# A routed feed-forward layer behind graph attention: which earlier sum tiles 4 and 5 wait for before they are added into the output

## The chip, the cores and the metric

The kernel runs on one core of a Trainium2 chip. The metric is the device time of one execution in microseconds (us); lower is better. The time before is the median of three runs.

## What is computed

```python
# x: (64, 128, 512), adj: (64, 128, 128), all fp32; 8192 tokens of 512 numbers
x = x + attention(layernorm(x), bias=adj + adj, Wq, Wk, Wv, Wo)    # 16 heads, within each block of 128 tokens

h = layernorm(x)                                                   # 8192 tokens
scores = maximum(h @ gate_W + gate_b, 1e-4)
p = softmax(scores)                                                # over 8 experts
topk_idx = top_k(p, 2)
w = maximum(p, 0.1) at the two chosen experts, divided by their sum
y = einsum('bsd,edf->bsef', h, expert_W) + expert_b
x = x + einsum('bsef,bse->bsf', y, comb) / 2                       # comb: w at the two chosen experts, else 0
```

## The kernel before

**Phase one** (`phase_a`) does the attention for 64 blocks of 128 tokens. It writes x after attention into the DRAM tensor `out`, and it scatters every normalised token twice into `x_lists`, once into the list of each of its two experts. A row of `x_lists` holds the 512 numbers, the token's number and its eight combination weights. At its end DVE fills the small table `tab` with three integers for each of the 135 tiles of phase two: the tile's expert, its first row in `x_lists`, and a count, described below.

**Phase two** (`phase_b`, L1201 to L1347) goes over the lists in 135 tiles of 128 rows (`TILES = 135`, 8192 x 2 / 128 = 128 and 7 spare ones), expert by expert. Below, tiles are counted from 0. Each engine has its own program, and the loops run over 6 tiles (`N`) per turn `g`, unrolled in Python; `tile(g, off)` is tile number 6g + off. There are 6 buffers for the gathered rows (`xg`) and their `token` and `comb`, and 3 (`R`) for `xgT_hi`, `xgT_lo`, `ps_x`, `ps_y` and `yt`.

- ACT gathers tile n into `xg` by a DMA (L1288), after a wait for the transposes and the `token` and `comb` copies of tile n-6 (L1286, L1287). In one step it first copies the transposed tile n from `ps_x` to `xgT_hi` (L1281) and then issues the gather of tile n+5.
- PE transposes tile n+2 into `ps_x` (L1266) between the three matmuls for each of four chunks of tile n into `ps_y` (L1260, L1261, L1262). Tile n's matmuls wait for `xgT_lo` of tile n (L1254) and for the addition of `yt` of tile n-3 (L1256).
- DVE takes in one step L1300 (`xgT_lo` = `ps_x` - `xgT_hi`) for tile n+2, then for tile n L1309 (`yt` = `ps_y` + bias, after a wait for the landing of the sum of tile n-3, whose buffer it takes, L1308) and L1312 (`yt` times the weight).
- POOL takes in one step the copies of `token` and `comb` for tile n+2 (L1330, L1331) and then the sum of tile n: an indirect DMA which adds the rows of `yt` into the rows `token` of `out` (L1343). It increments `added[n % 3]` by 16 when all of it has landed.

A token stands in two lists, so two sums of different experts can meet in a row of `out`, and an addition must not start before the other one has landed. Two tiles of one expert never share a token. The third number of `tab` says how far `added` of the previous tile's buffer must have come: 16 * ((n-1) // 3), which leaves the previous tile's own sum out, and 16 more where tile n-1 belongs to another expert, which takes it in. The value is at least 16 from tile 4 on. The wait order before each sum is:

```python
if t.after(2 * R):                       # L1335: from tile 6 on
    need = pool.value_load(tab[0:1, 2, bass.ds(t.count(), 1)], ...)
    hold(added[(j - 3) % R], 16 * tile(g, j - 3).turn(R) + 16)     # the sum of tile n-2 has landed
    hold(added[(j - 2) % R], need)                                 # what the table asks of tile n-1's buffer
elif t.after(1):                         # tiles 1 to 5
    pool.wait_ge(added[(j - 2) % R], 16 * tile(g, j - 2).turn(R) + 16)   # the sum of tile n-1 has landed
hold(y_step, t.count(2, 2))              # yt of tile n is complete
```

`hold` (L1317 to L1320) is a wait followed by an increment of a counter of POOL's own. The functions that the diff touches follow with the line numbers of the profile.

Of the kernel before, what the change touches and what calls it, by code (L numbers as in the profile page):

```python
# [1200 lines left out]
def phase_b(nc, v):  # L1201
# [5 lines left out]
    R = RING  # L1207
# [3 lines left out]
    with mem:  # L1211
# [20 lines left out]
        def tile(g, off):  # L1232
            return Item(g, N, off, TILES)

        def turns(body):
            for g in range(-1, TILES // N + 2):
                body(g)
# [3 lines left out]
        @block.tensor  # L1241
        def _(pe):
            def body(g):
                for j in range(N):

                    ahead, t = tile(g, j + 2), tile(g, j)
                    if ahead.valid:
                        pe.wait_ge(xg_in[ahead.ring(N)], 16 * ahead.turn(N) + 16)
                        if ahead.after(R):
                            pe.wait_ge(xgT_lo_done, ahead.count(1, 1 - R))  # L1250
                    if t.valid:
                        r = t.ring(R)
                        e = pe.value_load(tab[0:1, 0, bass.ds(t.count(), 1)], min_val=0, max_val=E - 1)
                        pe.wait_ge(xgT_lo_done, t.count(1, 1))  # L1254
                        if t.after(R):
                            pe.wait_ge(y_step, t.count(2, 1 - 2 * R))  # L1256
                    for c in range(DC):
                        if t.valid:
                            hi, lo = (we[:, bass.ds(e * (2 * DC * D) + (DC * i + c) * D, D)] for i in range(2))
                            nc.tensor.matmul(ps_y[r][:, :], xgT_hi[:, r, c, :], hi, start=c == 0, stop=False)  # L1260
                            nc.tensor.matmul(ps_y[r][:, :], xgT_hi[:, r, c, :], lo, start=False, stop=False)  # L1261
                            last = nc.tensor.matmul(ps_y[r][:, :], xgT_lo[:, r, c, :], hi, start=False, stop=c == DC - 1)  # L1262
                            if c == DC - 1:
                                last.then_inc(y_full, 1)
                        if ahead.valid:
                            last = nc.tensor.transpose(ps_x[ahead.ring(R)][:, P * c:P * c + P], xg[:, ahead.ring(N), P * c:P * c + P], ident)  # L1266
                            if c == DC - 1:
                                last.then_inc(xgT_full, 1)
            turns(body)
# [45 lines left out]
        @block.gpsimd  # L1315
        def _(pool):
            def hold(semaphore, value):  # L1317

                pool.wait_ge(semaphore, value)
                pool.sem_inc(poolb_held, 1)  # L1320

            def body(g):
                for j in range(N):
                    t = tile(g, j + 1)
                    if t.valid:
                        r, m = t.ring(R), t.ring(N)
                        hold(xg_in[m], 16 * t.turn(N) + 16)
                        if t.after(N):
                            hold(added[r], 16 * t.turn(R) - 16)
                        nc.gpsimd.tensor_copy(token[:, m, :], xg[:, m, D:D + 1]).then_inc(meta_done, 1)  # L1330
                        nc.gpsimd.tensor_copy(comb[:, E * m:E * m + E], xg[:, m, D + 1:W]).then_inc(meta_done, 1)  # L1331
                    t = tile(g, j - 1)
                    if t.valid:
                        r, m = t.ring(R), t.ring(N)
                        if t.after(2 * R):  # L1335

                            need = pool.value_load(tab[0:1, 2, bass.ds(t.count(), 1)], min_val=16, max_val=16 * (TILES // R + 1))
                            hold(added[(j - 3) % R], 16 * tile(g, j - 3).turn(R) + 16)
                            hold(added[(j - 2) % R], need)
                        elif t.after(1):  # L1340
                            pool.wait_ge(added[(j - 2) % R], 16 * tile(g, j - 2).turn(R) + 16)
                        hold(y_step, t.count(2, 2))
                        pool.indirect_dma_start(out=out, out_offset=bass.IndirectOffsetOnAxis(ap=token[:, m, :], axis=0),  # L1343
                                                in_=yt[:, r, :], in_offset=None, compute_op=ALU.add).then_inc(added[r], 16)
            turns(body)
            for r in range(R):
                pool.wait_ge(added[r], 16 * (TILES // R))  # L1347
# [42 lines left out]
```

## Time and profile before

| | |
|---|---|
| median of 3 runs | 1660.67 us (1660.43 to 1661.73) |
| the profiled execution | 1662.81 us |
| its span, first to last instruction | 1661.0 us |
| mean granted TensorE clock | 0.970 |
| PE busy | 1550.8 us (93%) |
| DVE, ACT, POOL busy | 1215.8, 955.9, 974.0 us |
| phase two | from about 1195 us on |
| sums into `out` (L1343), 135 | first at 1210.2, last at 1654.2 us |

The profile tells for each instruction when it started, how long it took and what ended the idle time of its engine before it. `PE` is the TensorE, `DVE` the VectorE, `ACT` the ScalarE, `POOL` the GpSimd. A granted clock of 1.00 is 2.4 GHz on the TensorE and 0.50 is 1.2 GHz. The duration of an indirect DMA on POOL is POOL's own work in issuing it; the transfer itself goes on behind it.

### The profile page before, as it was taken

The page shows a single profiled execution, that of the slowest core. Times are in us where ns is not written, and L with a number is a line of the kernel's source. Part 1 is how long each engine was busy: PE and PEld are TensorE (multiplying, and loading weights), DVE is VectorE, ACT ScalarE, POOL GpSimd, SP SyncE. Part 2 cuts the span into 40 slices and gives each one's busy share as a digit, 9 for nine tenths or more (in the row PEclk, how much of TensorE's full clock was granted, in tenths as well). Part 3 has the DMA queues.
Part 4 walks back from the last instruction along what each step waited for, and adds up shares of the span by engine and source line. Part 5 has one row for each costly group of instructions (what it writes and reads, how often), then busy time and mean ns, then how long its engine had stood idle before and what let it go on. Part 6 is the DMA issues. An engine that isn't in the chain of part 4 may idle for free. (4 is left out here: it accounts for less than half of the span.)

```text
span 1661.0 us, 45460 instructions
## 1 busy us (share of the span) xinstructions
PE 1550.8 (93%) x12808; PEld 1410.9 (85%) x12808; DVE 1215.8 (73%) x4952; ACT 955.9 (58%) x3129; POOL 974.0 (59%) x1788
## 2 busy tenths in 40 slices
PE   6999999999999999999999999966189999999996
PEld 6999999999999999999999999955167777777775
DVE  5578888888888888888888788877745555555554
ACT  4687777777777777777777777775111111111111
POOL 3255666566666666566665666556235565565655
PEclk9999999999999999999999999977599999999998
DMA  6787988789888888888887888794658898898886
GB/s 226 194 233 199 257 241 241 237 248 253 246 241 240 244 247 239 237 239 247 228 244 225 246 233 228 221 293 142 217 102 158 168 174 164 162 169 165 164 160 106
DMA packets 188629, 351.98 MB, mean 212 GB/s; under 512 B 20960, under 2 KB 30304, under 8 KB 188256
## 3 DMA queue, kind: packets, MB, share of 16 engines
q1 hardware_dynamic: 135520, 238.47, 51.7%
q0 software_dynamic: 29680, 69.55, 21.6%
q10 hardware_dynamic: 23184, 41.05, 8.0%
q8 instruction: 109, 1.79, 0.5%
q14 instruction: 136, 1.11, 0.2%
HBM read 189.48 MB, written 159.52 MB: 210 GB/s over the span
## 5 line engine op out<-in xcount | busy, mean ns | idle before, releaser
L678 ACT ACTIVATE prob<-prob,nmax 128x128 f32<-128x128 f32 x1024 | 398.8, 395 | 175.3 <-DVE amax L833 168.8
L1146 POOL TENSOR_TENSOR prob<-prob,rinv 128x512 f32<-128x512 f32 x256 | 261.4, 1042 | 241.3 <-DVE rinv L850 241.2
L829 DVE CUSTOM_DVE_ANT_0 prob<-ps_s,bias 128x128 f32<-128x128 f32 x1024 | 237.7, 287 | 142.1 <-PE ps_s L530 106.5
L1343 POOL DMA_INDIRECT out<-yt,token x135 | 211.6, 1567 | 196.3 <-DMA out<-yt,token 72.3
L1281 ACT ACTIVATE xgT_hi<-ps_x 128x512 fp32r<-128x512 f32 x135 | 80.7, 598 | 386.8 <-PE ps_x L1266 339.4
L1260 PE MATMUL ps_y<-we,xgT_hi 128*128 x540 | 260.8, 483 | 5.8 <-DVE xgT_lo L1300 5.8
L1261 PE MATMUL ps_y<-we,xgT_hi 128*128 x540 | 214.8, 398 | 0.0
L1262 PE MATMUL ps_y<-we,xgT_lo 128*128 x540 | 214.0, 396 | 0.0
L678 ACT ACTIVATION_READ_ACCUMULATOR prob<-prob,nmax 128x1 f32 x1024 | 196.7, 192 | 0.0
L833 DVE TENSOR_REDUCE amax<-prob 128x4 f32<-128x512 f32 x256 | 175.6, 686 | 8.9
L539 PE MATMUL ps_t<-const,prob 128*128 128x128 f32 x1024 | 164.8, 284 | 15.2 <-ACT pT L716 12.1
L1300 DVE TENSOR_TENSOR xgT_lo<-ps_x,xgT_hi 128x512 fp32r<-128x512 f32 x135 | 93.2, 690 | 105.6 <-ACT xgT_hi L1281 102.4
L1266 PE MATMUL ps_x<-const,xg 128*128 128x128 f32 x540 | 147.5, 276 | 21.1 <-DMA xg<-x_lists 21.1
L1156 POOL DMA_INDIRECT x_lists<-xn,pos x128 | 133.6, 1044 | 43.5 <-issue 37.7
L716 ACT ACTIVATE pT<-ps_t 128x512 f32<-128x512 f32 x256 | 152.1, 594 | 11.9 <-PE ps_t L539 9.7
L455 PE MATMUL ps_p<-xT_hi,wk_hi 128*128 128x256 f32 x512 | 150.9, 295 | 1.8 <-DVE xT_lo L815 1.8
L530 PE MATMUL ps_s<-ks,qs 96*128 96x128 f32 x1024 | 145.8, 265 | 7.2 <-issue 4.9
L1260 PEld LDWEIGHTS ps_y<-we,xgT_hi 128*128 128x128 f32 x540 | 102.7, 190 | 56.3 <-issue 9.3
L455 PE MATMUL ps_p<-xT_hi,wq_hi 128*128 128x256 f32 x512 | 149.7, 292 | 0.6 <-DVE kT_lo L802 0.6
L456 PE MATMUL ps_p<-xT_lo,wk_hi 128*128 128x256 f32 x512 | 145.8, 285 | 0.0
L457 PE MATMUL ps_p<-xT_hi,wk_lo 128*128 128x256 f32 x512 | 145.7, 285 | 0.0
L530 PEld LDWEIGHTS ps_s<-ks,qs 96*128 96x128 f32 x1024 | 138.7, 193 | 7.9 <-issue 7.7
(191 smaller groups left out, 4770.4 us busy)
## 6 DMA issues: line engine op xcount, KB each, us to landing
ks<-kq_parts SPq DMA_DIRECT2D x192, 256.0 KB, 4.2
qs<-kq_parts SPq DMA_DIRECT2D x192, 256.0 KB, 6.3
xg<-x_lists ACTq DMA_DIRECT2D x135, 260.5 KB
xin<-x SPq DMA_DIRECT2D x64, 256.0 KB, 7.2
kq_parts<-kT_hi SPq DMA_DIRECT2D x32, 512.0 KB, 3.8
kq_parts<-kT_lo SPq DMA_DIRECT2D x32, 512.0 KB, 4.8
kq_parts<-qT_hi SPq DMA_DIRECT2D x32, 512.0 KB
kq_parts<-qT_lo SPq DMA_DIRECT2D x32, 512.0 KB
```

Of the source, the lines that this page charges most:

```text
L455: mm(out_, lhs_hi, rhs_hi, start=first, stop=False)
L530: last = mm(ps_s[c % 2][:, P * h:P * h + P], qs[:, r, h, c, :], ks[:, r, h, c, :], start=True, stop=True)
L539: last = nc.tensor.transpose(ps_t[:, P * h:P * h + P], prob[:, b % 2, c, h, :], ident)
L678: last = nc.scalar.activation(prob[:, r, c, h, :], prob[:, r, c, h, :], ACT.Exp, bias=nmax[:, r, i:i + 1], scale=-1.0, accum_out=rsum[:, r ...
L716: nc.scalar.activation(pT[:, c].rearrange("p h t -> p (h t)"), ps_t[:, :], ACT.Copy).then_inc(pT_done, 1)
L829: last = nc.vector.tensor_tensor_reduce(out=prob[:, r, c, h, :], in0=ps_s[c % 2][:, P * h:P * h + P], in1=bias[:, b % 4, :], scale=-1.0, s ...
L833: nc.vector.tensor_reduce(amax[:, r, HC * c:HC * c + HC], prob[:, r, c, :, :], axis=AX.X, op=ALU.max, apply_absolute_value=True).then_inc( ...
L1146: tt(prob[:, r, q], prob[:, r, q], rinv[:, r, HC * q:HC * q + HC].unsqueeze(2).to_broadcast([P, HC, P]), ALU.mult)\
L1260: nc.tensor.matmul(ps_y[r][:, :], xgT_hi[:, r, c, :], hi, start=c == 0, stop=False)
L1261: nc.tensor.matmul(ps_y[r][:, :], xgT_hi[:, r, c, :], lo, start=False, stop=False)
L1262: last = nc.tensor.matmul(ps_y[r][:, :], xgT_lo[:, r, c, :], hi, start=False, stop=c == DC - 1)
L1343: pool.indirect_dma_start(out=out, out_offset=bass.IndirectOffsetOnAxis(ap=token[:, m, :], axis=0), in_=yt[:, r, :], in_offset=None, compu ...
```

## The change

The sums of tiles 4 and 5 take the branch that so far starts at tile 6. They wait for the landing of the sum of two tiles before and for the table's count, instead of the landing of the sum just before. Tiles 1 to 3 keep their wait, and nothing else changes.

```diff
@@ -1332,7 +1332,7 @@
                     t = tile(g, j - 1)
                     if t.valid:
                         r, m = t.ring(R), t.ring(N)
-                        if t.after(2 * R):
+                        if t.after(R + 1):
 
                             need = pool.value_load(tab[0:1, 2, bass.ds(t.count(), 1)], min_val=16, max_val=16 * (TILES // R + 1))
                             hold(added[(j - 3) % R], 16 * tile(g, j - 3).turn(R) + 16)
```

## Rows read from the trace of the kernel before

**Rows 1.** Who waited for whom, 1196 to 1661 us: total us, times, longest.

```profile
PE ps_x L1266 <- DMA xg<-x_lists: 21.1, 2, 20.8
PE ps_y L1260 <- DVE xgT_lo L1300: 5.8, 5, 2.2
```

**Rows 2.** Timeline of PE, starts of tiles 0, 7 to 12: start, us, instruction, [idle before].

```profile
1200.41 0.79 PE L1260 MATMUL ps_y<-we,xgT_hi 128*128 x1 [0.81 <-DVE xgT_lo L1300]
...
1225.82 0.50 PE L1260 MATMUL ps_y<-we,xgT_hi 128*128 x1 [0.17 <-DVE xgT_lo L1300]
...
1231.45 0.50 PE L1260 MATMUL ps_y<-we,xgT_hi 128*128 x1 [2.16 <-DVE xgT_lo L1300]
...
1236.11 0.41 PE L1266 MATMUL ps_x<-const,xg 128*128 128x128 f32 x1
1237.42 0.50 PE L1260 MATMUL ps_y<-we,xgT_hi 128*128 x1 [0.90 <-DVE xgT_lo L1300]
...
1242.72 0.50 PE L1260 MATMUL ps_y<-we,xgT_hi 128*128 x1 [1.79 <-DVE xgT_lo L1300]
...
1247.54 0.48 PE L1260 MATMUL ps_y<-we,xgT_hi 128*128 x1
...
1250.76 0.47 PE L1260 MATMUL ps_y<-we,xgT_hi 128*128 x1
```

**Rows 3.** Timeline of POOL, sums 3 to 6, 9, 14 and 15.

```profile
1227.44 1.56 POOL L1343 DMA_INDIRECT out<-yt,token  x1 [3.75 <-DMA out<-yt,token]
...
1233.12 1.55 POOL L1343 DMA_INDIRECT out<-yt,token  x1 [3.80 <-DMA out<-yt,token]
...
1238.69 1.56 POOL L1343 DMA_INDIRECT out<-yt,token  x1 [3.69 <-DMA out<-yt,token]
...
1240.74 1.56 POOL L1343 DMA_INDIRECT out<-yt,token  x1 [0.16 <-issue]
...
1252.01 1.56 POOL L1343 DMA_INDIRECT out<-yt,token  x1 [2.59 <-DMA out<-yt,token]
...
1266.35 1.56 POOL L1343 DMA_INDIRECT out<-yt,token  x1 [0.78 <-DVE yt L1309]
...
1272.29 1.55 POOL L1343 DMA_INDIRECT out<-yt,token  x1 [4.05 <-DMA out<-yt,token]
```

**Rows 4.** The chain that ended last: start, us, what.

```profile
1227.44 4.87 DMA out<-yt,token
...
1233.12 4.75 DMA out<-yt,token
...
1639.06 0.69 DVE xgT_lo L1300
...
1642.59 4.85 DMA out<-yt,token
```

**Rows 5.** Timeline of ACT, behind sum 5.

```profile
1240.80 0.35 ACTq L1288 DMA_DIRECT2D xg<-x_lists  x1
1241.26 0.60 ACT L1281 ACTIVATE xgT_hi<-ps_x 128x512 fp32r<-128x512 f32 x1 [4.70 <-PE ps_x L1266]
```

**Rows 6.** Timeline of DVE, L1312 of tile 4, L1309 of tiles 6, 8, 9.

```profile
1222.09 0.51 DVE L1312 TENSOR_SCALAR yt<-yt,comb 128x512 f32<-128x512 f32 x1 [0.21 <-DVE yt L1309]
...
1232.87 0.69 DVE L1309 TENSOR_TENSOR yt<-ps_y,e_bias 128x512 f32<-128x512 f32 x1 [1.56 <-DMA out<-yt,token]
...
1241.89 0.69 DVE L1300 TENSOR_TENSOR xgT_lo<-ps_x,xgT_hi 128x512 fp32r<-128x512 f32 x1 [2.40 <-ACT xgT_hi L1281]
1243.61 0.69 DVE L1309 TENSOR_TENSOR yt<-ps_y,e_bias 128x512 f32<-128x512 f32 x1 [1.03 <-DMA out<-yt,token]
...
1246.74 0.69 DVE L1309 TENSOR_TENSOR yt<-ps_y,e_bias 128x512 f32<-128x512 f32 x1 [1.14 <-DMA out<-yt,token]
```

**Rows 7.** Busy time by window: PE, PEld, DVE, ACT, POOL, granted clock, DMA share, GB/s.

```profile
1234.00:1236.00 2.00, 2.00 (x6) 1.41 (x6) 0.41 (x1) 0.04 (x1) 1.00 (x3) 0.50 0.46 38
...
1244.00:1246.00 2.00, 2.00 (x7) 1.51 (x7) 1.38 (x3) 0.00 (x0) 1.61 (x3) 0.50 0.91 227
```

## The prediction

> Tiles are counted from 0, so the "fifth tile" is tile 4. "Sum n" is the accumulating scatter of tile n into `out` (L1343), and "landed" means that its 16 counts are in. All times are microseconds from the start of the span.
>
> **What bounds the kernel now.** I read the page first: PE is busy for 93% of the span, so only places where PE waits can give anything back. The second view was who waits for whom in phase two. PE waits there for the first gathered rows and then five times for `xgT_lo`, 5.8 us in all and never over 2.2 [rows 1]. The PE timeline places these: 0.81 before tile 0, 0.17 before tile 7, then 2.16 before tile 8, 0.90 before tile 9 and 1.79 before tile 10 [rows 2]. Those make up the 5.8, so after tile 10 PE runs without a wait. A tile takes it 3.22 us (1247.54 to 1250.76).
>
> The third view, POOL's timeline, gives the reason [rows 3]. Sums 3, 4 and 5 start 5.68 and 5.57 apart, each after the landing of the one before it: the chain has 4.87 of DMA behind sum 3, 4.75 behind sum 4, and about 0.81 from landing to the next start [rows 4]. A beat of 5.65 against a PE that wants 3.22 makes POOL fall behind by 2.4 a tile until the slack of the rings is gone, which is at tile 8. From sum 6 on the sums wait for the one before the last: sum 6 starts 2.05 after sum 5. This is exactly the rule that the change brings to sums 4 and 5.
>
> How a sum holds PE: (a) by its start. POOL copies `token` and `comb` of tile n+3 behind sum n; ACT's gather of tile n+9 waits for them, and L1281 of tile n+5 is queued behind that gather. For sum 5: start 1238.69, gather 1240.80, L1281 1241.26, L1300 1241.89, PE tile 10 at 1242.72, so 4.03 from sum n to PE tile n+5 [rows 2, 3, 5]. (b) by its landing. DVE's L1309 of tile n+3 waits for it, and L1300 of tile n+6 is queued behind L1309 and L1312. From L1309 to the end of L1312 are 1.5, L1300 takes 0.69 and PE follows 0.14 later: about 2.35 from landing to PE tile n+6 [rows 6].
>
> **The change, part by part.** It touches two sums of 135. For each, one wait goes and two waits with their counter increments and one register load come; no compute instruction or DMA is added. No trace shows their cost by itself. It is inside the 2.05 from sum 5 to sum 6, where POOL runs just this program and its idle time before the sum is 0.16 [rows 3]: between nothing and 0.16 for each sum. I take the 2.05 as it stands; it hides under PE's tile 8, by the margins below, and if that cover were gone it would cost these 0.16. Behind these waits on POOL stand only the copies for the tiles three ahead, and behind them the gathers; all of them move forward with the sum.
>
> Does the table's count let tile 4 through? The count is 16 for tiles 4 and 5 (one landing on the semaphore of the previous tile's buffer) unless the expert changes there. Behind sum 6 the first sum that again waits for its direct predecessor is sum 15: 5.94 after sum 14, 4.05 of it idle [rows 3]. So expert 0 has 15 tiles. The landing asked for is that of sum 0 or 1; L1309 of tile 4 has waited for sum 1 already, and L1312 behind it ends at 1222.60 [rows 6]. So the count passes at once.
>
> New starts:
> - Sum 3 still waits for sum 2: 1227.44, as before.
> - Sum 4: 1227.44 + 2.05 = 1229.49 (before: 1233.12). Sum 2 has landed (sum 3 waited for it) and `yt` of tile 4 is ready since 1222.60.
> - Sum 5 waits for sum 3's landing, 1232.31, so 1233.12 (before: 1238.69). Whether sum 3 lands later with sum 4 beside it: sum 5, with sum 6 2.05 behind, has landed when L1309 starts at 1243.61, 4.9 after its start; alone a sum takes 4.75 to 4.87 [rows 4, 6]. I take no delay.
> - Sum 6 waits for sum 4. A second of a pair takes longer: sum 6 itself started at 1240.74 and L1309 of tile 9 at 1246.74, so 5.9. 1229.49 + 5.9 + 0.9 = 1236.3 (before: 1240.74).
> From here the sums repeat those of before two tiles later: sum n is old sum n+2 less 11.25 (1238.69 less 1227.44). That gives 1240.8 for sum 7, from the old sum 9 at 1252.01 [rows 3].
>
> New PE:
> - Tile 8 hangs on sum 3: 1231.45, with its 2.16 wait, unchanged. The granted clock is 0.50, the 1.2 GHz level, at 1234 to 1236 after it [rows 7]; this stays too, and tile 8 ends about 1236.52 (last transpose at 1236.11 plus 0.41).
> - Tile 9 could start by sum 3's landing at 1232.31 + 2.35 = 1234.7 and by sum 4's start at 1229.49 + 4.3 = 1233.8. PE is free at 1236.52, so it is PE that decides: 0.90 gained.
> - Tile 10: sum 5 gives 1233.12 + 4.03 = 1237.2, sum 4's landing 1235.4 + 2.35 = 1237.8; PE is free at 1236.52 + 3.23 = 1239.75. The 1.79 wait goes.
> - Without this wait the second slow stretch goes as well: PE tile 10 took 4.82 (1242.72 to 1247.54), with a granted clock of 0.50 at 1244 to 1246, against 3.22: 1.60.
> - Tiles 11 and 12: 1242.98 and 1246.21. Their limits are the landings of sums 5 and 6, 1233.12 + 5.9 + 2.35 = 1241.4 and 1236.3 + 5.9 + 2.35 = 1244.6. Both are covered.
>
> Sum: PE tile 12 starts at 1246.2 instead of 1250.76, **4.5 us** earlier: 0.90 + 1.79 + 1.60, and 0.27 because a PE wait in the trace begins at the end of the last, pipelined matmul, 0.27 longer than its turn. The cover of it all is PE's own work; what is late next is the wait at tile 8, which sum 3 (still serial) sets.
>
> Does it reach the end? The chain that ended last goes back from the last sums over L1312, L1309 and L1300 at 1639.06 into PE's matmuls [rows 4], which run unbroken back to tile 10. At the expert's end, sum 15 at 1272.29 + 4.03 = 1276.3 comes 0.3 before PE tile 20 needs it (1250.76 + 8 x 3.23 = 1276.6). By the two-tile shift the sums are then 4.5 to 5.3 earlier, so this margin does not shrink. I count all 4.5.
>
> The profiled execution took 1662.81, its span 1661.0; both lie above the median 1660.67. On its own span the forecast is 1656.5. Carried to the median: 1656.2.
>
> **A rule weighed.** The weakest term is the 1.60, since it rests on a single stretch of one execution. It has bounds of 0 (the clock does not fall in the run that counts) and 1.60 (it falls as here); a second fall that stays would be shorter, not longer. I take 1.60, the row itself. The Trainium skill, "TensorE: Matmul & The Clock Gate", "What's actually happening", says that what the gate watches runs free of the kernel and that slow matmuls therefore vary from run to run. By that rule the sum without the term would hold in some runs, 2.9.
>
> **The rivals.**
> 1. *The clock term is missing* from the timed runs of before: gain 0.90 + 1.79 + 0.27 = 2.96, time 1657.7. For it: the timed runs spread over 1.3 (1660.43 to 1661.73), about one such term, and the profiled one is above them. Against it: both waits over 1.7 us were followed by 1.2 GHz in the same execution. Chance 0.19.
> 2. *Sums in pairs share the DMA engines, and it ends slower.* If both of a pair land only after the two durations together, d = 9.7 after the first start, then PE tile 9 waits until 1227.44 + 9.7 + 2.35 = 1239.5, sum 5 starts at 1238.0 and tile 11 at 1238.0 + 9.7 + 2.35 = 1250.0, 2.5 later than the old 1247.54; with another slow stretch, 1.60, that is 4.1 slower, 1664.8. It decides from 2d + 1230.6 = 1247.54, d = 8.5. Against it: the pair of sums 5 and 6 took 4.9 and 5.9. The Trainium skill, "DMA: Bandwidth & Descriptors", "Issuing engines are not separate DMA queues", says that all DMAs "run on the same 16 DMA engines and interleave with each other". Chance 0.03.
> 3. *Sum 3 lands 3 late beside sum 4 and the gather of tile 12*, 7.9 after its start. Then tile 9 waits until 1235.3 + 2.35 = 1237.65 and tile 10 starts at 1240.9, 1.8 before the old one, and the 1.1 of waiting brings the second slow stretch back: gain 1.8, time 1658.9. For it: L1309 of tile 6 started 0.56 after the landing that the chain shows [rows 4, 6]. Against it: the pair of sums 5 and 6, and that the wait of 0.90 before tile 9 had no 1.2 GHz behind it. Chance 0.10.
> 4. *The change does nothing*, because the table asks tiles 4 and 5 for more than one landing: 1660.7. Against it stands expert 0's length. Chance 0.02.
>
> **How the numbers follow.** About 0.2%, 3.3 us, is what a measurement of this kernel can tell from no change. The forecast (gain 3.4 to 5.8, centre 4.5) has 0.66; its upper end adds a slow stretch more in before. Rival 1 straddles the line of 3.3: 0.04 of its 0.19 counts as faster. Faster: 0.66 + 0.04 = 0.70. Same: 0.15 + 0.10 + 0.02 = 0.27. Slower: 0.03. The range takes the forecast's upper end of 5.8 (1654.9) and reaches over rival 1 with 0.9 of spread (1658.6), which leaves out rival 3, the tail of rival 1 and the two small ones, under 0.2.
>
> **What would show it.** Sum 4 at about 2.05 after sum 3, sum 5 at 5.7 after sum 3, sum 6 3.2 behind that. PE waits 3.1 in five or fewer pieces, with 2.16 before tile 8 left and none before tiles 9 and 10. One stretch at 1.2 GHz after 1230 instead of two. PE tile 12 near 1246.2. Wrong: a wait before tile 10, a landing of sum 3 over 6 us, or a new PE wait near tile 20.

## The result

The changed kernel took 1658.51 us (median of 22 runs, 1655.07 to 1662.07); the kernel before, run beside it, 1662.90 (22 runs, 1659.46 to 1665.48). The ratio is 0.9976 with a 95% interval of 0.9968 to 0.9983: 4.0 us faster, 2.8 to 5.3. Two later comparisons of the same two kernels gave 0.9985 (0.9975 to 0.9995) and 0.9981 (0.9968 to 0.9993), so 2.5 and 3.2 us.

The forecast was 1656.2, 4.5 us faster than the first median of 1660.67. The sign and the mechanism came out. The number did not: the 1660.67 rested on three runs, and 22 runs of the same kernel have their median 2.2 higher. Set against the old 1660.67 the changed kernel's 1658.51 shows only 2.2 of gain. Set against the kernel run beside it the gain is 4.0, but that this comes so near to 4.5 is in part luck: over the three comparisons, weighted by their intervals, I estimate a gain of 3.4.

| | before | after |
|---|---|---|
| median, 22 runs each | 1662.90 us | 1658.51 us |
| profiled execution, span | 1662.81, 1661.0 us | 1658.36, 1656.6 us |
| PE's waits for `xgT_lo` | 5.8 us in 5 | 3.0 us in 3 |
| start of PE tile 0 | 1200.41 | 1199.69 |
| PE tile 7 to tile 12, start to start | 24.94 us | 20.04 us |
| PE's last tile to the end of the span | 16.7 us | 18.0 us |

Who waited for whom in phase two, the changed kernel; it answers to [rows 1]:

```profile
PE ps_x L1266 <- DMA xg<-x_lists: 21.2, 2, 20.8
PE ps_y L1260 <- DVE xgT_lo L1300: 3.0, 3, 2.0
```

POOL's timeline, sums 2 to 7 of the changed kernel; it answers to [rows 3]:

```profile
1220.99 1.56 POOL L1343 DMA_INDIRECT out<-yt,token  x1 [3.74 <-DMA out<-yt,token]
...
1226.51 1.56 POOL L1343 DMA_INDIRECT out<-yt,token  x1 [3.64 <-DMA out<-yt,token]
...
1228.56 1.56 POOL L1343 DMA_INDIRECT out<-yt,token  x1 [0.16 <-issue]
...
1232.28 1.56 POOL L1343 DMA_INDIRECT out<-yt,token  x1 [1.83 <-DMA out<-yt,token]
...
1235.17 1.56 POOL L1343 DMA_INDIRECT out<-yt,token  x1 [1.00 <-DVE yt L1309]
...
1237.99 1.56 POOL L1343 DMA_INDIRECT out<-yt,token  x1 [0.93 <-DVE yt L1309]
```

Sum 4 now starts 2.05 after sum 3 instead of 5.68, to the hundredth what was forecast, and sum 5 follows 5.77 after sum 3 (forecast 5.68).

PE's timeline, the starts of tiles 7, 8, 9, 10 and 12 in the changed kernel; it answers to [rows 2]:

```profile
1225.01 0.50 PE L1260 MATMUL ps_y<-we,xgT_hi 128*128 x1 [0.22 <-DVE xgT_lo L1300]
...
1230.53 0.50 PE L1260 MATMUL ps_y<-we,xgT_hi 128*128 x1 [2.04 <-DVE xgT_lo L1300]
...
1235.25 0.58 PE L1260 MATMUL ps_y<-we,xgT_hi 128*128 x1
...
1238.58 0.48 PE L1260 MATMUL ps_y<-we,xgT_hi 128*128 x1
...
1245.05 0.48 PE L1260 MATMUL ps_y<-we,xgT_hi 128*128 x1
```

The wait before tile 8 is still there (2.04), those before tiles 9 and 10 are gone, and no wait has come in their place. The busy times by window (columns as in [rows 7]) show one stretch at the 1.2 GHz level behind the wait at tile 8, and none from there to PE's last tile at 1638.64:

```profile
1232.00:1234.00 2.00, 2.00 (x8) 1.45 (x7) 1.79 (x3) 0.00 (x0) 1.72 (x3) 0.51 0.88 220
1234.00:1236.00 2.00, 2.00 (x8) 1.51 (x8) 1.33 (x3) 0.37 (x1) 0.99 (x3) 0.64 0.87 106
1236.00:1238.00 2.00, 2.00 (x12) 1.56 (x11) 1.38 (x2) 0.23 (x1) 1.07 (x4) 1.00 1.07 205
```

DVE's timeline shows the two landings of the pair, since L1309 of tiles 6, 7 and 8 waits for sums 3, 4 and 5; it answers to [rows 6]:

```profile
1231.86 0.69 DVE L1309 TENSOR_TENSOR yt<-ps_y,e_bias 128x512 f32<-128x512 f32 x1 [1.47 <-DMA out<-yt,token]
...
1234.39 0.69 DVE L1309 TENSOR_TENSOR yt<-ps_y,e_bias 128x512 f32<-128x512 f32 x1 [0.23 <-DMA out<-yt,token]
...
1237.19 0.69 DVE L1309 TENSOR_TENSOR yt<-ps_y,e_bias 128x512 f32<-128x512 f32 x1 [0.24 <-DMA out<-yt,token]
```

Sum 3 to this L1309 is 5.35 (5.43 before the change), sum 4 is 5.83, sum 5 is 4.91. Two sums in flight cost the second one about 1 us here and the first one nothing. The size varies: for the second of a pair that starts 2.05 behind the first, the distance is 5.80 and at most 5.4 to 5.7 in the other traces of this kernel, 5.34 in the kernel with only tile 5 changed, and 5.5 to 6.5 for sum 6 in four traces of the kernel before.

Between the two traces PE gains 4.90 from tile 7 to tile 12 and phase one happened to end 0.72 sooner; 1.2 of this is lost again behind PE's last tile, and the span is 4.4 shorter. So the profiled 4.4, too, agrees with 4.5 only because these two happen to cancel nearly. The experiments ask which of these belong to the change.

### The profile page after: what moved, and what is told of

Its sections match the earlier page's. It is cut to its first block and busy times, and to the rows that moved or that the text cites. A ratio compares the mean times of both kernels' runs of the same rounds, so it can differ in the third digit from the quotient of the medians.

```text
span 1656.6 us, 45470 instructions
## 1 busy us (share of the span) xinstructions
PE 1549.9 (94%) x12808; PEld 1411.3 (85%) x12808; DVE 1216.8 (73%) x4952; ACT 963.0 (58%) x3129; POOL 975.5 (59%) x1788
## 3 DMA queue, kind: packets, MB, share of 16 engines
q8 instruction: 109, 1.79, 0.5%
## 5 line engine op out<-in xcount | busy, mean ns | idle before, releaser
L457 PE MATMUL ps_p<-xT_hi,wq_lo 128*128 128x256 f32 x512 | 145.4, 284 | 0.0
```

Of the source, the lines that this page charges most:

```text
L457: return mm(out_, lhs_lo, rhs_hi, start=False, stop=last)
```

## Experiments

Times in the texts below are counted from the start of PE tile 0 where they say so. That distance contains tile 0 itself, which takes between 4.57 and 5.98 in these traces. As a measure that is free of this and of phase one I use the distance from the start of PE tile 7 to that of tile 12; with no wait and a full clock it is 16.15 (5 tiles of 3.23). The "tail" is the distance from the start of PE's last tile to the end of the span. Every ratio is to the kernel before, run beside the experiment.

**Only tile 5 changed.** To the kernel before:

```diff
-                        if t.after(2 * R):
+                        if t.after(R + 2):
```

> Only tile 5 leaves the serial wait; tile 4 keeps it. Theory of the shift (each tile freed early moves all later sums by one pair rule, PE waits for sum n-5's start and sum n-6's landing): sum 5 starts 2.05 us after sum 4 instead of 5.6, PE's waits before tiles 8 (about 2.1) and 9 (0.9) stay, the one before tile 10 goes. PE tile 12 starts 47.0 to 47.5 us after PE tile 0 (50.35 in before, 45.36 in the changed kernel), so 60 to 75% of the change's gain: ratio 0.9980 to 0.9988. Rival (only tile 4's wait is worth anything, tile 5's is hidden): no change, ratio 1.000.

Ratio 0.9987 (0.9978 to 0.9996), 2.2 us faster. Tile 7 to 12 took 20.88. Sum 5 started 2.04 after sum 4, and PE waited before tiles 8 and 9 but no longer before tile 10. PE's timeline, tiles 8, 9, 10 and 12:

```profile
1228.27 0.50 PE L1260 MATMUL ps_y<-we,xgT_hi 128*128 x1 [1.90 <-DVE xgT_lo L1300]
1234.14 0.49 PE L1260 MATMUL ps_y<-we,xgT_hi 128*128 x1 [2.37 <-DVE xgT_lo L1300]
...
1237.35 0.48 PE L1260 MATMUL ps_y<-we,xgT_hi 128*128 x1
...
1243.77 0.48 PE L1260 MATMUL ps_y<-we,xgT_hi 128*128 x1
```

PE tile 12 came at 45.90 after tile 0, sooner than the 47.0 to 47.5 that I had written; 0.64 of this lies ahead of tile 8, where nothing was changed. The clock did not fall here, neither behind 1.90 nor behind 2.37 of waiting, and tile 10 followed tile 9 by 3.21, a full-speed tile. A fall behind the 1.90 would not have shown at tile 12: tile 9 starts 5.87 after tile 8 here and 5.97 in [rows 2], since with the slow stretch its wait is 0.90 and without it 2.37. Sum 4's start sets tile 9, and a slow stretch behind tile 8 is hidden under that wait. The rival falls: freeing tile 5 alone is worth more than half of the change (2.3 of about 3.1 at PE, 23.2 to 20.88), since a single freed sum already starts the pairs. Freeing tile 4 too brings another 0.8 at PE (20.88 to 20.04) where the clock falls behind tile 8, which then nothing hides, and 1.95 where it does not (18.93, the third trace of the changed kernel).

**Pairs from tile 2 on**, to the changed kernel:

```diff
+                        elif t.after(2):
+                            pool.wait_ge(added[(j - 3) % R], 16 * tile(g, j - 3).turn(R) + 16)
                         elif t.after(1):
```

> Tiles 2 and 3 too wait for the sum of two tiles before (a constant in place of the table's count, which is enough as long as expert 0 has at least four tiles). Theory of the shift: the PE waits before tiles 7 (0.2) and 8 (2.1) go, and the stretch at 1.2 GHz behind tile 8 as well (1.2 to 1.6); PE tile 12 starts 41.3 us after PE tile 0 (45.36 in the changed kernel, 50.35 in before). If all of it reaches the end: 9 us under before, ratio 0.9946. Rival (the end is set by the loop of sums behind the last change of expert, not by PE): PE tile 12 as said, but the span shrinks by less than 6 us, ratio 0.9965 or more.

Ratio 0.9954 (0.9941 to 0.9968), 7.6 us faster than before. Tile 7 to 12 took 16.15, the full speed. Of PE's waits for `xgT_lo` one is left, ahead of tile 0:

```profile
PE ps_y L1260 <- DVE xgT_lo L1300: 0.8, 1, 0.8
```

This confirms that the serial sums cause PE's waits up to tile 10, the one of tile 8 among them, and that PE's gain arrives at the end: here the wait before tile 7 goes as well, so PE's gain is counted from tile 6. From there to tile 12 it takes 19.37 and, in the traces of before without the second slow stretch, 26.9 to 27.1: 7.5 to 7.7 at PE, 7.6 in the timed runs. The run moves sums 2 and 3 together; that tile 8 hangs on sum 3's start and not on sum 2's landing rests on the arithmetic of the prediction, not on this run. Tile 12 came at 40.35 after tile 0, 0.9 sooner than I had written, and the 9 us were too many, since they were counted from the first trace, with its second slow stretch.

**Pairs from tile 1 on**, to the kernel with pairs from tile 2. The serial branch goes altogether; sum 1 waits for no sum.

```diff
-                        elif t.after(1):
-                            pool.wait_ge(added[(j - 2) % R], 16 * tile(g, j - 2).turn(R) + 16)
```

> Every sum up to tile 5 follows the rule of two tiles before; sum 1 waits for no sum at all. In the trace of the kernel with pairs from tile 2 PE has no wait left behind tile 0, so PE decides. Theory of the cover: sum 1 starts 2.5 to 3 us sooner, PE tile 12 stays at 40.3 us after tile 0 and the ratio stays at 0.9954, within 0.0007. Rival (the sums still set the pace through the end): 0.9940 or less.

Ratio 0.9947 (0.9934 to 0.9960), tile 7 to 12 again 16.15. PE tile 12 was at 40.12 against 40.35 after tile 0; sum 1 moved from 15.02 to 11.82 and no one needed it. With PE covered, an earlier sum is worth nothing that these runs can tell.

**PE kept at work in its waits**, to the kernel before; results unused:

```diff
+                    for _ in range({8: 15, 9: 5, 10: 12}.get(N * g + j, 0)):
+                        nc.tensor.transpose(ps_f[:, 0:P], ident, ident)
                     if t.valid:
                         r = t.ring(R)
```

> The kernel before, with 15, 5 and 12 transposes of a constant (results unused) put on PE ahead of its waits for tiles 8, 9 and 10, so that PE has work for most of the 2.16, 0.90 and 1.79 us in which it would be idle; no sum moves. Theory (1.6 us of the forecast are the clock's fall after such a wait): no stretch at 1.2 GHz after tile 8 and after tile 10, PE tile 12 starts 1.6 to 3.2 us sooner after PE tile 0 than the 50.35 of before (tile 8's stretch is partly hidden under the next wait), ratio about 0.9988. Rival (the clock's fall is not tied to the idle time, or is hidden): the clock falls all the same, PE tile 12 at 50.35 or later, ratio 1.000 to 1.001.

Ratio 1.0004 (0.9995 to 1.0013), where I had written 0.9988. In the trace both stretches at 1.2 GHz were gone, and PE tile 12 came at 47.76 after tile 0, 2.6 sooner than in the first trace but no sooner than the 47.65 of the third trace of before. PE's waits before tiles 8, 9 and 10, and the window after the last of them:

```profile
1228.31 0.50 PE L1263 MATMUL ps_y<-we,xgT_hi 128*128 x1 [0.23 <-DVE xgT_lo L1303]
1234.10 0.49 PE L1263 MATMUL ps_y<-we,xgT_hi 128*128 x1 [1.74 <-DVE xgT_lo L1303]
1239.30 0.50 PE L1263 MATMUL ps_y<-we,xgT_hi 128*128 x1 [0.44 <-DVE xgT_lo L1303]
```

```profile
1240.00:1242.00 2.00, 2.00 (x12) 1.55 (x11) 1.33 (x3) 0.47 (x1) 0.76 (x1) 1.00 1.02 195
```

Yet the timed runs gained nothing; the interval allows 0.8 us at most. So in the timed runs of before there was little of this clock loss to remove, unless the added work costs as much elsewhere, which no run separates. That is the first sign against the 1.60 of the forecast.

**The opposite dose: serial up to tile 8.** To the kernel before:

```diff
-                        if t.after(2 * R):
+                        if t.after(3 * R):
```

> The opposite dose: tiles 6, 7 and 8 get the serial wait as well (the kernel before has it up to tile 5). Theory of the shift: sums 6, 7, 8 start 5.65 us apart, each such tile costs PE 5.65 less 3.0 to 3.2 us and leaves a wait of 1.5 to 2.4 us before each of tiles 11, 12 and 13; PE tile 16 comes 6 to 10 us later than in before, and the time is 4 to 9 us longer, ratio 1.003 to 1.005. Rival (the startup is absorbed later, since the sums catch up): within 2 us of before, ratio 1.001 or less.

Ratio 1.0052 (1.0039 to 1.0066), 8.6 us slower. Sums 6, 7 and 8 started 5.35, 5.26 and 5.30 behind the one before each, and PE now waited before tiles 11 and 12 as it does before tile 10:

```profile
1243.30 0.50 PE L1260 MATMUL ps_y<-we,xgT_hi 128*128 x1 [1.60 <-DVE xgT_lo L1300]
1248.64 0.49 PE L1260 MATMUL ps_y<-we,xgT_hi 128*128 x1 [1.86 <-DVE xgT_lo L1300]
1253.90 0.49 PE L1260 MATMUL ps_y<-we,xgT_hi 128*128 x1 [1.78 <-DVE xgT_lo L1300]
```

Behind the 1.60 and the 1.86 the next tile came at full speed (5.34 and 5.26 later, wait included). Of these three only the 1.78 had slow matmuls behind it, and they took up the third wait that I had written: 0.24 is left of it before tile 13. The startup is not absorbed later. PE's tiles 7 to 14 took 35.35 instead of 29.7 to 31.4, 4 to 6 more. Tile 16 came 3.8 to 6.5 later after tile 0 than in the traces of before, not the 6 to 10 that I had written, and both are less than the 8.6 of the timed runs; where the rest went stays open.

**More traces of the two kernels.** Unchanged copies.

> The kernel before, unchanged, for a second trace. Theory A (the second stretch at 1.2 GHz of the forecast is an accident of single executions): it can be missing here behind PE's wait before tile 10, and PE tile 12 then starts 48.5 to 49 us after tile 0 instead of 50.35. Theory B (it always follows such a wait): slow matmuls again right behind that wait, tile 12 at 50.0 to 50.5. Ratio 1.000 either way.

Ratio 0.9995 (0.9985 to 1.0006). PE's timeline, tiles 8, 9, 10, 11 and 12:

```profile
1229.40 0.50 PE L1260 MATMUL ps_y<-we,xgT_hi 128*128 x1 [2.02 <-DVE xgT_lo L1300]
1235.32 0.50 PE L1260 MATMUL ps_y<-we,xgT_hi 128*128 x1 [0.85 <-DVE xgT_lo L1300]
1240.55 0.49 PE L1260 MATMUL ps_y<-we,xgT_hi 128*128 x1 [1.72 <-DVE xgT_lo L1300]
1243.81 0.48 PE L1260 MATMUL ps_y<-we,xgT_hi 128*128 x1
1247.04 0.48 PE L1260 MATMUL ps_y<-we,xgT_hi 128*128 x1
```

Nearly the same wait before tile 10 as in [rows 2], 1.72 against 1.79, and tile 11 follows 3.26 later, not 4.82. Theory A holds: tile 12 at 48.35. The window from 1242, where the first trace has its second fall, has a granted clock of 1.00:

```profile
1242.00:1244.00 2.00, 2.00 (x12) 1.55 (x11) 1.28 (x3) 0.00 (x0) 1.71 (x3) 1.00 0.89 227
1244.00:1246.00 2.00, 2.00 (x12) 1.55 (x11) 1.68 (x3) 0.60 (x1) 1.26 (x4) 1.00 0.86 95
```

In this trace PE does not run without a wait behind tile 10, as it did in the first. It waits 0.43 before tile 13, 0.44 before tile 20, 0.55 before tile 33 and 1.23 before tile 126, 8.1 in 9 instead of 5.8 in 5, and from tile 12 to the last tile it needs 397.4 instead of 393.5. The clock fell behind none of these:

```profile
1618.97 0.50 PE L1260 MATMUL ps_y<-we,xgT_hi 128*128 x1 [1.23 <-DVE xgT_lo L1300]
```

> The kernel before, unchanged, for a third trace: is there a stretch at 1.2 GHz behind PE's wait before tile 10? So far one trace of two. With it PE tile 12 at 50.0 to 50.5 us after tile 0, without it 48.3 to 48.8.

Tile 12 at 47.65 after tile 0, tile 11 3.23 behind tile 10: no second stretch again.

> The changed kernel, unchanged, for a second trace. PE tile 12 at 45.0 to 45.6 us after tile 0 under the theory of the shift, with a wait of 1.9 to 2.2 before tile 8 alone. Theory that the tail of the first trace (17.96 us from PE's last tile to the end, against 16.6 to 16.8 in five other kernels) was an accident of landings: 16.5 to 16.9 here, and the span is 5 us under that of before when counted from PE tile 0. Rival (the change moves the tail): 17.5 or more again. Ratio 0.997 to 0.998.

Ratio 0.9985, above the 0.997 to 0.998 that I had written. Tile 12 at 45.44. PE waited 1.26 before tile 126 here too, so such late waits come with either kernel. The tail was 18.96, the number that I had given to the rival (the change moves the tail); but the second and third trace of before have 19.79 and 19.24, so a long tail comes without the change as well.

> The changed kernel, unchanged, for a third trace and a third ratio. PE tile 12 at 45.2 to 45.5 us after tile 0 as in both traces so far. Ratio between the two so far, 0.9976 and 0.9985: if the gain is 0.90 + 1.79 + 0.27 = 2.96 us and the slow stretch is rare in before, 0.9980 to 0.9983; if it is common, 0.9972 to 0.9976.

Ratio 0.9981 (0.9968 to 0.9993), tile 12 at 44.83; here the clock did not fall behind the 2.12 of waiting at tile 8 and a wait of 0.20 before tile 9 remained. PE's timeline, tiles 8 and 9:

```profile
1232.67 0.49 PE L1260 MATMUL ps_y<-we,xgT_hi 128*128 x1 [2.12 <-DVE xgT_lo L1300]
...
1236.34 0.49 PE L1260 MATMUL ps_y<-we,xgT_hi 128*128 x1 [0.20 <-DVE xgT_lo L1300]
```

Tile 9 follows 3.67 behind tile 8, and 4.72 in the first trace. In the kernel before, tile 9 starts 5.92 to 5.97 behind tile 8 with this stretch or without it. So the change takes away the cover of the first slow stretch, and where the clock does not fall behind tile 8 the change is worth 1.1 to 1.3 more.

**The tail.** Sums left out of the output, to the changed kernel (tiles 124 and 126) and then to both kernels (124 and 125):

```diff
+                        if N * g + j - 1 in (124, 126):
+                            pool.dma_start(v["kq_parts"][0, (N * g + j - 1 - 124) // 2, 0, :, 0:8], yt[:, r, 0:8]).then_inc(added[r], 16)
+                            continue
```

> The changed kernel with the sums of tiles 124 and 126 left out of the output (a small DMA to scratch stands in their place and does the counting). It gives the loop of sums behind the last change of expert 4 to 6 us of slack. Theory (in some executions of the changed kernel this loop, not PE, holds the last sums): the tail from PE's last tile is 16.5 to 16.8, never near 18, and the time is 0.3 to 1 us under the changed kernel's, ratio to before 0.9965 to 0.9975. Rival (PE sets the end always): the same ratio as the changed kernel's, within 0.0003.

> The kernel before with the sums of tiles 124 and 125 left out of the output (a small DMA to scratch does their counting), so that both strands of the sums behind the last change of expert, the even and the odd one, are cut and get 5 to 6 us of slack. Theory (in the executions whose tail is over 17 us the sums, not PE, hold the last stretch, in both kernels alike): the tail from PE's last tile to the end is 16.5 to 16.8 us, the time 0.5 to 1.5 us under before, ratio 0.9990 to 0.9997. Rival (PE sets the end in before): ratio 1.000, tail 16.7 as in the first trace.

> The changed kernel with the sums of tiles 124 and 125 left out in the same way. Tail 16.5 to 16.8 us instead of 17.96 and 18.96. Set beside the kernel before with the same two left out, the difference is PE's own gain at the start, 2.95 us without and 4.9 us with the second stretch at 1.2 GHz. Theory (that stretch is missing in most executions, and the tail takes about 1 us more from the changed kernel than from before): ratio to before 0.9970 to 0.9976, 3 to 4 us between the two. Rival (the tail takes the same from both): the difference of the two equals that of the full kernels, 2.5 to 4 us, and both gain the same by leaving the pair out.

The first of these left out the wrong pair: each sum waits for the one two before, so even and odd tiles form two strands, and 124 and 126 cut only the even one. Its tail was 17.72, its ratio 0.9976 (0.9965 to 0.9987), which tells neither theory from the other. With both strands cut, before gave 0.9996 (0.9985 to 1.0007) with a tail of 16.65, and the changed kernel 0.9970 (0.9959 to 0.9982) with a tail of 17.16 (expected 16.5 to 16.8). The difference of the two is 0.0026, 4.3 us. The intervals are too wide to say that the change pays anything in the tail.

All traces together (us; the last tile is PE tile 134; the slow stretches are those at 1.2 GHz behind the wait of tile 8 and behind a later one):

| kernel | tile 7 to 12 | first slow stretch | second slow stretch | last tile to end |
|---|---|---|---|---|
| before, three traces | 24.94, 23.13, 23.29 | yes, yes, yes | yes, no, no | 16.7, 19.8, 19.2 |
| before, pair left out | 23.25 | no | no | 16.7 |
| changed, three traces | 20.04, 20.20, 18.93 | yes, yes, no | no, no, no | 18.0, 19.0, 17.1 |
| changed, pair left out | 20.05 | yes | no | 17.2 |
| changed, 124 and 126 left out | 20.20 | yes | no | 17.7 |
| only tile 5 | 20.88 | no | no | 16.6 |
| pairs from tile 2, from tile 1 | 16.15, 16.15 | no, no | no, no | 16.8, 19.4 |
| before, PE kept at work | 22.87 | no | no | 16.6 |
| serial up to tile 8 | 26.78 | yes | yes, behind tile 12 | 16.6 |

The tail swings between 16.7 and 19.8 with the kernel before and between 17.1 and 19.0 with the changed one, so the 1.2 lost there between the first two traces is not shown to be the change's.

## Why the prediction was right or wrong

- **The rule of the pairs** (sum 4 at +2.05, sum 5 at +5.7): right, 2.05 and 5.77. Further on the two-tile shift is less exact: sum 7 started 11.5 after sum 3, where the forecast had 13.4 from a single old sum; PE was covered, and nothing hung on it.
- **The landings** (no delay for the first of a pair, 5.9 for the second): right, 5.35, as in before (5.43), and 5.83. Rivals 2 and 3 fall with it. The Trainium skill, "DMA: Bandwidth & Descriptors", "Issuing engines are not separate DMA queues", says that all DMAs run on the same engines and interleave with each other. The 1 us that the second pays fits that; no run shows that sharing is its cause.
- **The waits before tiles 9 and 10**, 0.90 + 1.79 + 0.27 = 2.96: right. Traces of before without the second slow stretch take 23.1 to 23.3 from tile 7 to 12, those of the changed kernel mostly 20.0 to 20.2, so 3.1 less. The kernel with only tile 5 changed and the two with earlier pairs show from both sides that it is these waits. In the first pair of traces PE gained 4.90, not 4.56: 0.35 of it is that tile 9, with no wait before it, starts 4.72 behind tile 8 and not 5.07. The forecast counted the overlap of a wait with the last matmul (its 0.27) at tile 10 alone.
- **The table's count lets tiles 4 and 5 pass**: right. Rival 4 falls.
- **The wait at tile 8 stays and is late next**: right, 2.04, and the pairs from tile 2 take it away.
- **The first slow stretch stays**: in four of five traces of the changed kernel, as in three of four of before. The forecast held it for a constant. In before it is hidden, in the changed kernel it costs 1.1 to 1.3 (20.04 to 20.20 against 18.93).
- **The clock term, 1.60**: this step failed. "I take 1.60, the row itself" made a rule out of one stretch of one execution. The second stretch stands in one of four traces with before's sums at the start (the fourth with the pair left out near the end), and keeping PE at work through the waits gained at most 0.8 in the timed runs. Weighted by the four traces the term is 0.4, and the gain 2.96 + 0.4 = 3.4, inside all three measured intervals (4.0, 2.5 and 3.2); the means of the traces, 23.65 and 19.88 from tile 7 to 12, differ by 3.8. Four traces are few, and the forecast's 4.5 lies outside one of the three intervals only (0.8 to 4.2). Rival 1, at 0.19, describes three of the four traces. The Trainium skill, "TensorE: Matmul & The Clock Gate", "What's actually happening", says that the number of slow matmuls at a kernel's start varies from run to run; here the slow stretches in the middle of the kernel do so too.
- **Carried to the median**: this step failed as well, and it makes nearly all of the miss in the absolute number. The profiled run lay 2.1 above a median of three runs, and I carried the forecast away from it to that median; with 22 runs it lies on the median (1662.81 against 1662.90). So the forecast's 1656.2 started from a base that was 2.2 too low; with the right base it would have been 1658.4, against 1658.51 measured. The 1658.51 lies at the upper end of the recorded range (1658.6), where the prediction had placed rival 1. The first comparison alone therefore does not speak against the clock term; the further traces, PE kept at work and the other two comparisons do. The range was made of the change's terms only and had nothing in it for the base. In the other comparisons the median of before was 1660.34, 1664.34 and 1663.23.
- **Does it reach the end**: yes within what can be told, 7.6 for 7.5 to 7.7 at PE in the kernel with pairs from tile 2. That PE runs unbroken from tile 10 on holds in the first trace and not in the second (0.43, 0.44, 0.55 and 1.23 of later waits). A wait near tile 20, one of the signs of being wrong, stands in two of four traces of before (0.44 and 0.16) and in none of the changed kernel, so the margin of 0.3 there was thin before the change already.

## What to carry to other kernels

A rule that holds for the steady state and is replaced by a stricter one for the first few tiles costs more than it seems: the serial beat (5.65) against the consumer's (3.22) builds a backlog that shows up as stalls four or five tiles later, where nothing looks serial. Every strict tile that is freed gives its part (2.2 us for tile 5, about 3.4 for tiles 4 and 5, 7.6 for tiles 2 to 5), and once the consumer has no wait left nothing more is to be had. A stall can also be the cover of a slow stretch before it, which the change then lays open. A stretch of low clock seen once in a trace is a term with a probability: look for it in a second trace, and take the base from as many runs as the size of the effect asks for.

The best version tried has pairs from tile 1 or 2, 0.9947 and 0.9954 of before, against 0.9976 for this change. Its constants hold only if the first expert has at least four tiles; here it has 15.

## What the hardware showed

- The granted clock fell to the 1.2 GHz level behind PE waits between 1.78 and 2.20 (1.78, 1.79, 1.84, 2.02, 2.04, 2.10, 2.16 twice, 2.18, 2.20), and not behind 1.23, 1.26, 1.60, 1.72 twice, 1.74, 1.77, 1.86, 1.90, 1.98, 2.12, 2.37 and 2.44 in other places and executions. Between 1.78 and 2.44 the length of the wait does not decide.
- Most sums in the chains of these traces land 4.5 to 5.1 us after their start, and now and then one needs more (5.85 for the one at 1300.59 in the second trace of before). In the same trace a wait of POOL for a landing, near the end, had 2.71 where its neighbours had about 1:

```profile
1635.23 1.56 POOL L1343 DMA_INDIRECT out<-yt,token  x1 [0.90 <-DVE yt L1309]
...
1639.84 1.56 POOL L1343 DMA_INDIRECT out<-yt,token  x1 [2.71 <-DMA out<-yt,token]
```

  This execution has a tail of 19.8, and the one with pairs from tile 1, which has a like wait of 2.50, one of 19.4. The other two long tails, 19.2 and 19.0, have no wait of POOL of this size there, so it is not the whole account of them. What delays these landings was not found.
- The runs of one kernel, where there are ten or more, spread over 5 to 9 us. The tails, 16.6 to 19.8, are one part of it. A larger part lies ahead of phase two: PE tile 0 starts anywhere from 1197.87 to 1203.04 in the fourteen traces. Over the 22 runs of the changed kernel the time goes with the mean granted clock: the two runs at 0.967 took 1661.5 on average, the eleven at 0.970 1658.4 and the two at 0.972 1656.7. The traces do not settle which of the two follows the other.
